# A Mamba layer with routed experts on one core: the skip term u*D scaled on ScalarE and added by turns on TensorE, batches 1 to 5

## Chip, cores and metric

One core of one Trainium2 chip. The metric is the device time of one execution in microseconds. The kernel before took 610.64 us, the median of 3 runs (609.68 to 610.68).

## What is computed

The input x is [8, 512, 128]: eight batches of 512 tokens. The layer returns x plus a Mamba block plus a mixture of experts, both on the normalised x. All arithmetic of the block is in fp32.

```python
xz = xn @ in_proj_w.T                       # x_s, z: 256 channels each
u = silu(causal_conv4(x_s) + conv_b)        # [b, t, 256]
delta = softplus(dt_raw @ dt_proj_w.T + dt_proj_b)
h = exp(delta * A) * h + delta * u * B_t    # 16 states per channel, a scan over t
y = sum over states of h * C_t  +  u * D_param
out = (y * silu(z)) @ out_proj_w.T + residual
```

The experts: two of eight for each token, each `(silu(x @ gate) * (x @ up)) @ down`, weighted and added. The change concerns the term `u * D_param`.

## The kernel before

**Layout.** Channels lie on the 128 partitions in two halves, hf = 0 and 1, and the 512 tokens of a batch along the free dimension. `u_sb[b % 3]` holds u of batch b as [128, 2, 512]; `d_sb` holds D_param as one column for each half.

**Order of the work.** Each engine has its own list, written out by hand, in batches b of 16 steps; step k is state k of the scan. In batches 1 to 5 one step has, on VectorE: the scan of half 0 (line 1144), the first gating product of an expert tile (line 1188), the product with C of half 0 (line 1161), the scan of half 1, the second gating product (line 1195), the product of half 1. ScalarE makes the decays exp(delta * A) into two PSUM banks by turns (`decay_bank`, line 515), each of which waits until the product that read the bank is done; it also moves the expert tile's results: `out_out` (line 714), `gate_out` (line 707) and `slots_out` (lines 696 and 700). Its list in a step is: decay of half 1, `out_out`, the work of `early`, the z gate in two steps, the decay of the next step's half 0, `gate_out`, `slots_out`, the work of `late`. In step 9 it takes the logarithm of the softplus for the next batch (line 770), with a table load before and another behind it, ahead of the decay of the next step and of `out_out`. Steps 8 and 14 have the two halves of tanh for the convolution of batch b + 2.

TensorE has in a step, in this order: the down projection of the tile before (`down`, line 1584), `up` (line 1598), `accumulate` (line 1433), the skip if there is one, `gate` (line 1592), `slots_turn` (line 1576), then convolutions, projections and the like. More exactly the skip of batches 1 to 5 comes once, in step 9 (`SKIP_AT`), behind `gate` and ahead of `slots_turn`; the latter waits for `out_out` of the tile before.

**Sum over states.** `accumulate` turns the products of one state (8 matmuls of 128x128 against the identity, with is_transpose) and adds them in two PSUM banks, `HT[0]` and `HT[1]`, which then hold y by time: tokens on partitions, channels along the free dimension. y stays there over the 16 steps.

**The skip.** `skip(b)` adds u * D_param into the same banks: 8 plain matmuls of u with `dd_sb[:, hf, :]`, a diagonal matrix of D_param that GpSimd makes at the start:

```python
MM(HT[i][:, t % 2, hf * P:(hf + 1) * P], u_sb[b % 3][:, hf, t * P:(t + 1) * P], dd_sb[:, hf, :],
   start=False, stop=False, skip_group_check=True)
```

Batches 0, 6 and 7 do it in other steps, in two parts. All of u_sb[b % 3] has other readers before step 6 of batch b only: the projection to B, C and dt (line 1482) and delta * u (line 457), both done for batch b while batch b - 1 runs. Its next writer is the convolution of batch b + 3.

**Other users of an engine's time.** `keep` (line 1341) issues matmuls whose result nobody reads; it stands in the steps of batches 0, 1, 5, 6 and 7 that have no expert tile. GpSimd makes dbu (line 931) and SyncE's queue brings expert weights, four tiles ahead, and rows of B and C.

Of the kernel before, what the change touches and what calls it, by code (L numbers as in the profile page):

```python
# [8 lines left out]
ACT = mybir.ActivationFunctionType  # L9
# [3 lines left out]
def build(nc, x, norm_w, w_in, conv_w, conv_b, x_proj, dt_proj, dt_b, a_log, d_par, w_out,  # L13
# [9 lines left out]
    P = 128  # L23
# [32 lines left out]
    with ctx:  # L56
        def sb(name, shape, dt=FP32):
            return ctx.enter_context(nc.sbuf_tensor(name, shape, dt))

        def sem(name):  # L60
            return ctx.enter_context(nc.semaphore(name))


        id_sb = sb("id_sb", [P, P])
# [8 lines left out]
        dd_sb = sb("dd_sb", [P, NH, P])  # L73
        dtb_sb = sb("dtb_sb", [P, NH])
        a_sb = sb("a_sb", [P, NH, S])
        d_sb = sb("d_sb", [P, NH])
# [52 lines left out]
        u_sb = [sb(f"u_sb{i}", [P, NH, T]) for i in range(3)]  # L129
# [27 lines left out]
                  for i in range(2)]  # L157
# [27 lines left out]
        HT = [bank[2 + q][:, :].rearrange("p (a c) -> p a c", a=2) for q in range(2)]  # L185
# [10 lines left out]
                   first1 first2 first3 first4 first5 first6 first7 both0 both1 both2 both3 both4 both5 both6 both7 part_mm comb dbuT_a sp_corr a_ready stats_bn st rms_rt xn_w xh_w  # L196
                   xh_pe xhT_c lgmm oh_out rt top_rdy sel_rdy tot_mm tot_out rk_out slot_rdy texp_rdy lohi_rdy lo_rdy hi_set hi_rdy map_mm src_rdy
                   exp_rt x_pad acc_w g_mm u_mm bct_rdy dbu_p row_mm dbu_0 b_st b_in0 b_in1 c_in0 c_in1
                   br_mm dbu_rdy da_rdy h_rdy p_rdy acc_mm y_out dd_rdy xc_mm x_th x_half u_rdy v_mm
                   v_out bc_mm bc_rdy z_mm z_rdy z_one o_ev sp_exp sp_ln sp_rem sp_w sp_sum z_th delta_rdy du_rdy  # L200
                   dut_mm dut_rdy yb_mm g_rdy o_mm o_rdy o_out""".split()
        s = {k: sem(k) for k in names}
# [12 lines left out]
        def tile(g):  # L215

            return TILE.get(g)
# [50 lines left out]
        def z_step(b):  # L268

            return {13: 1, 15: 0} if b == 0 else {7: 1, 11: 0} if b == 6 else {4: 1, 6: 0}  # L270
# [190 lines left out]
        def _(act):  # L461
# [32 lines left out]
            def decay(n):  # L494

                b, k = n // S, n % S
                i = IN_SBUF.index(n)
                for hf in range(NH):
                    if i >= ND:
                        act.wait_ge(s["h_rdy"], 2 * IN_SBUF[i - ND] + hf + 1)  # L500
                    if k == 0:
                        act.wait_ge(s["delta_rdy"], 2 * b + hf + 1)
                    nc.scalar.activation(da_of(n)[:, hf, :], delta[b % 2][:, hf, :], ACT.Exp,  # L503
                                         scale=a_sb[:, hf, k:k + 1]).then_inc(s["da_rdy"], 1)

            def decay_bank(n, hf):

                b, k = n // S, n % S
                m = 2 * k + hf
                wait(act, "p_rdy", freed(b, m))  # L510
                if b == 6 and m == 2:
                    act.wait_ge(s["dut_rdy"], 3)
                if k == 0:
                    act.wait_ge(s["delta_rdy"], 2 * b + hf + 1)
                nc.scalar.activation(bank_of(b, m)[:, :], delta[b % 2][:, hf, :], ACT.Exp,  # L515
                                     scale=a_sb[:, hf, k:k + 1]).then_inc(s["da_rdy"], 1)
# [18 lines left out]
            def input_turned(i):  # L535

                if i == 1:
                    act.wait_ge(s["o_rdy"], 5)
                for c in range(2):
                    act.wait_ge(s["dut_mm"], 2 * i + c + 1)  # L540
                    at = bank[2 + c] if i == 0 else FB[1 - c]
                    nc.scalar.activation(duT[:, 2 * c:2 * c + 2, :], at[:, :].rearrange("p (a c) -> p a c", a=2),
                                         ACT.Copy).then_inc(s["dut_rdy"], 1)
# [35 lines left out]
            def step(b, k):  # L579

                g = b * S + k
                prev, here, nxt, nn = tile(g - 1), tile(g), tile(g + 1), tile(g + 2)
                more = b < NB - 1
                if b < 6:
                    decay_bank(g, 1)
                elif b == 6:
                    if k == 0:
                        decay_bank(g, 1)
                        y_evac(b - 1)
                        input_turned(1)  # L590
                    if k + 1 < S and g + 1 not in BY_PE:
                        decay_bank(g + 1, 0)
                elif k == 0:
                    decay(g + 1)
                if k == 0 and b != 6:
                    y_evac(b - 1)
                if b == NB - 1 and k == TURNED + 2:
                    y_evac(b)
                if b == 7:
                    if k + 2 < S:  # L600
                        decay(g + 2)
                    if k == 0:
                        input_turned(2)
                    elif k + 1 < S:
                        scaled(g + 1)
                if b < 6 and k == LOG_AT[b]:
                    logarithm(b + 1)
                if prev is not None and not (b < 6 and k == LOG_AT[b]):
                    out_out(prev)
                if more:  # L610
                    early(b, k)
                if b != 6 and k in z_step(b):
                    z_gate(b, k)
                if b == 6 and k + 2 < S and g + 2 in BY_PE:
                    scaled(g + 2)
                if b < 6:
                    decay_bank(g + 1, 0)
                    if k == LOG_AT[b] and prev is not None:
                        out_out(prev)
                elif b == 6 and k + 1 < S and g + 1 not in BY_PE:  # L620
                    decay_bank(g + 1, 1)
                elif b == 6 and k + 1 == S:
                    decay_bank(g + 1, 0)
                    decay_bank(g + 1, 1)
                if nxt is not None:
                    gate_out(nxt)
                if nn is not None:
                    slots_out(nn)
                if b == 6 and k + 2 < S and g + 2 in BY_PE:
                    decay(g + 2)  # L630
                if more:
                    late(b, k)
                if b == 6 and k in z_step(b):
                    z_gate(b, k)

            def early(b, k):

# [22 lines left out]
            def z_gate(b, k):  # L660

                i, hf = z_turn(b, k), z_step(b)[k]
                if i == 0:
                    wait(act, "g_rdy", 2 * b)
                act.wait_ge(s["z_mm"], 2 * b + i + 1)
                if 0 < b < 6:
                    if i == 0:
                        act.wait_ge(s["z_rdy"], 2 * b)
                        wait(act, "o_rdy", b - 1)
                    if b == 1:  # L670
                        act.wait_ge(s["dbuT_a"], S - 1)
                    nc.scalar.activation(du_t[:, hf, :], z_bank(b)[:, :], ACT.Copy)
                nc.scalar.activation(zs_sb[:, hf, :], z_bank(b)[:, :], ACT.Tanh, scale=0.5).then_inc(s["z_th"], 1)
                if 0 < b < 6:
                    act.wait_ge(s["z_th"], 2 * b + i + 1)
                    nc.scalar.activation(zs_sb[:, hf, :], zs_sb[:, hf, :], ACT.Identity, bias=sign_sb[:, 0:1]).then_inc(s["z_one"], 1)

            def projected(b):

                act.wait_ge(s["o_mm"], b + 1)  # L680
                act.wait_ge(s["z_rdy"], 2 * b + 3)
                nc.scalar.activation(du_t[:, 1, :], FB[0][:, :], ACT.Copy).then_inc(s["o_ev"], 1)

            def y_evac(b):

                last = (b + 1) * S if b < NB - 1 else (NB - 1) * S + TURNED + 1
                for i in range(2):
                    wait(act, "acc_mm", 2 * last - 1 + i)
                    at = y_sb if b < NB - 1 else y_end
                    nc.scalar.activation(at[:, 2 * i:2 * i + 2, :], HT[i], ACT.Copy).then_inc(s["y_out"], 1)  # L690
# [643 lines left out]
        def _(pe):  # L1334
            MM = nc.tensor.matmul
# [102 lines left out]
            def skip(b, banks=(0, 1)):  # L1438

                if b == 0:  # L1440
                    pe.wait_ge(s["dd_rdy"], NH)
                for i in banks:
                    for t in (2 * i, 2 * i + 1):
                        for hf in range(NH):
                            last = MM(HT[i][:, t % 2, hf * P:(hf + 1) * P], u_sb[b % 3][:, hf, t * P:(t + 1) * P], dd_sb[:, hf, :],
                                      start=False, stop=False, skip_group_check=True)

            def conv(c, hf, taps):

# [273 lines left out]
            for hf in range(NH):  # L1723
# [3 lines left out]
               start=True, stop=True).then_inc(s["row_mm"], 1)  # L1727
# [15 lines left out]
            for hf in range(NH):  # L1743
                pe.wait_ge(s["g_rdy"], 2 * (NB - 1) + hf + 1)
                for i in range(2):
                    for t in (2 * i, 2 * i + 1):
                        last = MM((GB, UB)[i][:, (t % 2) * H:(t % 2 + 1) * H], g_sb[:, hf, t * P:(t + 1) * P], wo_sb[:, hf, :],
                                  start=False, stop=(hf == NH - 1), skip_group_check=True)
# [66 lines left out]
```

## Time and profile before

| | |
|---|---|
| median of 3 runs | 610.64 us (609.68 to 610.68) |
| profiled execution | 611.13 us, its span 609.3 us |
| VectorE (DVE) busy | 588.5 us, 97%, 852 instructions |
| TensorE (PE) busy | 542.0 us, 89%, 3554 |
| GpSimd (POOL) busy | 494.1 us, 81%, 389 |
| ScalarE (ACT) busy | 455.0 us, 75%, 916 |
| mean granted TensorE clock | 0.969 of full speed |

The span runs from the first to the last instruction; the profiled execution's time has 1.8 us more around it. Busy is the time in which the engine had an instruction running. Successive instructions of one engine overlap a little in the records, and a matmul's recorded length includes its way through the array. A fp32 matmul stands as several records where it needs several passes. L1445 is line 1445 of the kernel; "idle before" names what released the instruction.

### The profile page before, as it was taken

The page shows a single profiled execution, that of the slowest core. Times are in us where ns is not written, and L with a number is a line of the kernel's source. Part 1 is how long each engine was busy: PE and PEld are TensorE (multiplying, and loading weights), DVE is VectorE, ACT ScalarE, POOL GpSimd, SP SyncE. Part 2 cuts the span into 40 slices and gives each one's busy share as a digit, 9 for nine tenths or more (in the row PEclk, how much of TensorE's full clock was granted, in tenths as well). Part 3 has the DMA queues.
Part 4 walks back from the last instruction along what each step waited for, and adds up shares of the span by engine and source line. Part 5 has one row for each costly group of instructions (what it writes and reads, how often), then busy time and mean ns, then how long its engine had stood idle before and what let it go on. Part 6 is the DMA issues. An engine that isn't in the chain of part 4 may idle for free.

```text
span 609.3 us, 11382 instructions
## 1 busy us (share of the span) xinstructions
PE 542.0 (89%) x3554; PEld 422.5 (69%) x3554; DVE 588.5 (97%) x852; ACT 455.0 (75%) x916; POOL 494.1 (81%) x389
## 2 busy tenths in 40 slices
PE   5999889898898998999989999899999797778887
PEld 2387766656787777877887777877777465657564
DVE  6999989999999999999999999999999998999997
ACT  1789697259857888579876698767985589969880
POOL 5693466569999799998999889998998967885784
PEclk9889798979999999999999999999999899988999
DMA  7430119725787887878868888688884455333364
GB/s 205 135 130 1 74 36 223 306 82 157 256 304 223 293 289 223 311 226 296 296 190 304 291 288 279 203 300 268 280 266 156 156 195 210 110 99 98 88 137 90
DMA packets 60893, 122.99 MB, mean 202 GB/s; under 512 B 8218, under 2 KB 41378, under 8 KB 53794
## 3 DMA queue, kind: packets, MB, share of 16 engines
q1 hardware_dynamic: 53826, 112.42, 54.7%
q0 software_dynamic: 6288, 9.52, 7.3%
q8 instruction: 29, 0.48, 0.3%
q10 hardware_dynamic: 720, 0.33, 0.2%
q14 instruction: 30, 0.25, 0.1%
HBM read 112.77 MB, written 9.47 MB: 201 GB/s over the span
## 4 chain that ended last, share of the span: by engine, by line
PE 50%; DVE 19%; ACT 16%; issue 13%; POOL 1%; DMA 1%; DVEq 0%; ACTq 0%; POOLq 0%
PE bank L1433 9%; PE bank L1584 8%; PE bank L1467 8%; DVE bank L1144 8%; PE bank L1598 6%; DVE h_sb L1161 6%; PE bank L1592 5%; ACT bank L515 3%; ACT dbu L531 3%; PE bank L1490 2%; ACT da L503 2%; PE bank L1482 2%; PE bank L1396 1%; PE bank L1565 1%; ACT L770 1%
## 5 line engine op out<-in xcount | busy, mean ns | idle before, releaser
L931 POOL TENSOR_TENSOR dbu<-du,xn_all 128x1024 f32<-128x1024 f32 x86 | 203.7, 2369 | 24.9 <-DVE bank L1144 21.5
L1144 DVE TENSOR_TENSOR_SCAN bank<-bank,dbu 128x512 f32<-128x512 f32 x170 | 207.4, 1222 | 0.8 <-ACT bank L515 0.2
L1161 DVE TENSOR_TENSOR h_sb<-bank,xh_all 128x512 f32<-128x512 f32 x240 | 159.6, 680 | 1.2
L515 ACT ACTIVATE bank<-delta,a_sb 128x512 f32<-128x512 f32 x170 | 116.7, 688 | 37.9 <-DVE h_sb L1161 37.2
L1433 PE MATMUL bank<-id_sb,h_sb 128*128 128x128 f32 x992 | 131.9, 277 | 10.9 <-DVE h_sb L1161 9.3
L1433 PEld LDWEIGHTS bank<-id_sb,h_sb 128*128 128x128 f32 x992 | 112.9, 143 | 21.6 <-DVE h_sb L1161 14.7
L1144 DVE TENSOR_TENSOR_SCAN bank<-da,bank 128x512 f32<-128x512 f32 x82 | 96.0, 1215 | 4.6 <-PE bank L1396 2.9
L1584 PEld LDWEIGHTS bank<-wd_sb,hid 117*128 117x128 f32 (+1 forms) x432 | 54.8, 191 | 49.2 <-DVE hid L1195 28.4
L1584 PE MATMUL bank<-wd_sb,hid 117*128 117x128 f32 (+1 forms) x432 | 64.1, 284 | 18.7 <-ACT xT L696 17.2
L915 POOL DMA_INDIRECT xs<-xn_rows,src x72 | 69.8, 970 | 12.5 <-issue 9.9
L531 ACT ACTIVATE dbu<-du_t,bc_sb 128x256 f32<-128x256 f32 x164 | 69.4, 496 | 6.3 <-PE bank L1396 3.4
L1396 PE MATMUL bank<-id_sb,dbu 128*128 128x128 f32 x328 | 53.1, 288 | 15.1 <-DVE h_sb L1161 9.2
L1396 PEld LDWEIGHTS bank<-id_sb,dbu 128*128 128x128 f32 x328 | 39.6, 148 | 35.2 <-issue 23.7
L1467 PE MATMUL bank<-xhT,wk_sb 128*128 128x512 f32 x128 | 62.9, 619 | 0.7 <-ACT xhT L474 0.7
L503 ACT ACTIVATE da<-delta,a_sb 128x512 f32<-128x512 f32 x86 | 58.3, 714 | 5.0 <-DVE bank L1144 4.9
L1592 PE MATMUL bank<-xT,wgu_sb 128*118 128x128 f32 x432 | 59.3, 274 | 0.4 <-DVE ga L1188 0.2
L1598 PE MATMUL bank<-xT,wgu_sb 128*118 128x128 f32 x432 | 59.0, 272 | 0.0
L707 ACT ACTIVATE th<-bank 118x384 f32<-118x384 f32 x72 | 34.8, 483 | 26.8 <-PE bank L1592 25.9
L981 POOL DMA_INDIRECT xhT<-y_slots,slot x40 | 38.6, 965 | 19.0 <-DVE bank L1144 7.8
L1598 PEld LDWEIGHTS bank<-xT,wgu_sb 128*118 128x118 f32 x432 | 52.7, 182 | 0.5 <-issue 0.5
L1592 PEld LDWEIGHTS bank<-xT,wgu_sb 128*118 128x118 f32 x432 | 52.3, 182 | 0.9 <-issue 0.8
L714 ACT ACTIVATE ys<-bank,stat 128x128 f32<-128x128 f32 x72 | 26.2, 364 | 29.1 <-PE bank L1584 29.0
(198 smaller groups left out, 893.8 us busy)
## 6 DMA issues: line engine op xcount, KB each, us to landing
xh_all<-b_rows SPq DMA_DIRECT2D x30, 1024.0 KB, 7.5
xn_all<-b_rows SPq DMA_DIRECT2D x25, 1024.0 KB
wgu_sb<-in_w_gu SPq DMA_DIRECT2D x72, 352.0 KB
wd_sb<-in_w_dn SPq DMA_DIRECT2D x72, 192.0 KB
y_slots<-ys SPq DMA_DIRECT2D x72, 64.0 KB
xn_rows<-xn_all SPq DMA_DIRECT2D x2, 1040.0 KB, 11.4
out<-x_sb SPq DMA_DIRECT2D x7, 256.0 KB, 7.0
x_sb<-in_x SPq DMA_DIRECT2D x2, 640.0 KB, 6.0
```

Of the source, the lines that this page charges most:

```text
L503: nc.scalar.activation(da_of(n)[:, hf, :], delta[b % 2][:, hf, :], ACT.Exp, scale=a_sb[:, hf, k:k + 1]).then_inc(s["da_rdy"], 1)
L515: nc.scalar.activation(bank_of(b, m)[:, :], delta[b % 2][:, hf, :], ACT.Exp, scale=a_sb[:, hf, k:k + 1]).then_inc(s["da_rdy"], 1)
L531: last = nc.scalar.activation(dbuT[k % 2][:, t, :], duT[:, t, :], ACT.Copy, scale=bc_sb[q][:, t, k:k + 1])
L931: nc.gpsimd.tensor_tensor(dbu[k % 2][:, :, :], du[b % 2][:, :, :], b_ring[c % 2][:, k % CH, :].unsqueeze(1).to_broadcast([P, NH, T]), ALU. ...
L1144: nc.vector.tensor_tensor_scan(at, da_of(n)[:, hf, :] if n in IN_SBUF else at, inp, 0.0, ALU.mult, ALU.add).then_inc(s["h_rdy"], 1)
L1161: nc.vector.tensor_tensor(h_sb[k % 2][:, hf, :], bank_of(b, 2 * k + hf)[:, :], row, ALU.mult).then_inc(s["p_rdy"], 1)
L1396: last = nc.tensor.transpose(at[:, t * P:(t + 1) * P], dbuT[k % 2][:, t, hf * P:(hf + 1) * P], id_sb[:, :])
L1433: last = MM(HT[i][:, t % 2, hf * P:(hf + 1) * P], h_sb[k % 2][:, hf, t * P:(t + 1) * P], id_sb[:, :], is_transpose=True, start=(k == 0 and ...
L1467: last = MM(at[:, :], wk_sb[:, tap, hf * P:(hf + 1) * P], xhT[:, c, tap:tap + T], start=(tap == taps[0] if c == 0 else tap == 0), stop=(ta ...
L1584: last = MM(XD[:, P:P + H], hid[j % 2][0:FN[c], c * P:(c + 1) * P], wd_sb[j % NW][0:FN[c], c, :], start=(c == 0), stop=(c == NF - 1))
L1592: last = MM(GB[0:FW, c * P:(c + 1) * P], wgu_sb[j % NW][:, c * FS:c * FS + FW], xT[j % 2][:, :], start=True, stop=True)
L1598: last = MM(UB[0:FW, c * P:(c + 1) * P], wgu_sb[j % NW][:, F + c * FS:F + c * FS + FW], xT[j % 2][:, :], start=True, stop=True)
```

## The change

In batches 1 to 5, ScalarE multiplies u_sb[b % 3] in place by the column of D_param, one 128x512 half at the end of step 6 and one at the end of step 7. In step 9 TensorE waits for both and adds u with the identity and is_transpose, as `accumulate` does, in place of the product with the diagonal matrix. Batches 0, 6 and 7 stay as they are. A semaphore, `us_rdy`, is new.

```diff
@@ -632,6 +632,8 @@
                     late(b, k)
                 if b == 6 and k in z_step(b):
                     z_gate(b, k)
+                if 0 < b < 6 and k in (6, 7):
+                    skip_input(b, k - 6)
 
             def early(b, k):
 
@@ -680,6 +682,13 @@
                 act.wait_ge(s["o_mm"], b + 1)
                 act.wait_ge(s["z_rdy"], 2 * b + 3)
                 nc.scalar.activation(du_t[:, 1, :], FB[0][:, :], ACT.Copy).then_inc(s["o_ev"], 1)
+
+            def skip_input(b, hf):
+
+                act.wait_ge(s["br_mm"], b + 1)
+                act.wait_ge(s["du_rdy"], 2 * b + hf + 1)
+                nc.scalar.activation(u_sb[b % 3][:, hf, :], u_sb[b % 3][:, hf, :], ACT.Copy,
+                                     scale=d_sb[:, hf:hf + 1]).then_inc(s["us_rdy"], 1)
 
             def y_evac(b):
 
@@ -1439,11 +1448,14 @@
 
                 if b == 0:
                     pe.wait_ge(s["dd_rdy"], NH)
+                if 0 < b < 6:
+                    pe.wait_ge(s["us_rdy"], 2 * b)
                 for i in banks:
                     for t in (2 * i, 2 * i + 1):
                         for hf in range(NH):
-                            last = MM(HT[i][:, t % 2, hf * P:(hf + 1) * P], u_sb[b % 3][:, hf, t * P:(t + 1) * P], dd_sb[:, hf, :],
-                                      start=False, stop=False, skip_group_check=True)
+                            MM(HT[i][:, t % 2, hf * P:(hf + 1) * P], u_sb[b % 3][:, hf, t * P:(t + 1) * P],
+                               id_sb[:, :] if 0 < b < 6 else dd_sb[:, hf, :], is_transpose=0 < b < 6,
+                               start=False, stop=False, skip_group_check=True)
 
             def conv(c, hf, taps):
 
```

## Rows read from the trace of the kernel before

**Rows 1.** The page: busy us of each engine with shares of the span, and the granted clock

```profile
PE 542.0 (89%) x3554; PEld 422.5 (69%) x3554; DVE 588.5 (97%) x852; ACT 455.0 (75%) x916; POOL 494.1 (81%) x389
...
PEclk9889798979999999999999999999999899988999
```

**Rows 2.** A stretch within batches 1 to 5: length, busy us (instructions) PE, PEld, DVE, ACT, POOL, clock

```profile
140.00:470.00 330.00, 304.23 (x2261) 256.52 (x2260) 329.10 (x454) 257.75 (x543) 303.71 (x195) 1.00 0.78 263
```

**Rows 3.** Groups by form: line, engine, operation, count, busy us, mean ns of one

```profile
L1433 PE MATMUL bank<-id_sb,h_sb 128*128 128x128 f32 x992 | 131.9, 277 | 10.9 <-DVE h_sb L1161 9.3 <-DVE g_sb L1169 1.5
...
L1445 PE MATMUL bank<-dd_sb,u_sb 128*128 128x128 f32 x128 | 16.9, 284 | 0.0
...
L734 ACT ACTIVATE u_sb<-u_sb,sign_sb 128x512 f32<-128x512 f32 x14 | 10.1, 723 | 0.5
```

**Rows 4.** Timeline, ScalarE, batch 2, steps 6 to 8: start, length, instruction, idle before

```profile
224.48 0.38 ACT L700 ACTIVATE stat<-xs,stat 128x1 f32<-128x1 f32 x1
224.80 0.69 ACT L515 ACTIVATE bank<-delta,a_sb 128x512 f32<-128x512 f32 x1
225.67 0.37 ACT L714 ACTIVATE ys<-bank,stat 128x128 f32<-128x128 f32 x1 [0.18 <-PE bank L1584]
226.98 0.69 ACT L515 ACTIVATE bank<-delta,a_sb 128x512 f32<-128x512 f32 x1 [0.94 <-DVE h_sb L1161]
...
229.16 0.69 ACT L515 ACTIVATE bank<-delta,a_sb 128x512 f32<-128x512 f32 x1 [0.38 <-DVE h_sb L1161]
230.35 0.37 ACT L714 ACTIVATE ys<-bank,stat 128x128 f32<-128x128 f32 x1 [0.50 <-PE bank L1584]
```

**Rows 5.** Timeline, VectorE, batch 2, steps 7 to 11

```profile
226.87 1.22 DVE L1144 TENSOR_TENSOR_SCAN bank<-bank,dbu 128x512 f32<-128x512 f32 x1
...
231.23 1.22 DVE L1144 TENSOR_TENSOR_SCAN bank<-bank,dbu 128x512 f32<-128x512 f32 x1
...
238.62 1.23 DVE L1144 TENSOR_TENSOR_SCAN bank<-bank,dbu 128x512 f32<-128x512 f32 x1
...
246.41 0.54 DVE L1195 TENSOR_TENSOR hid<-ga,bank 118x384 f32<-118x384 f32 x1
```

**Rows 6.** Timeline, ScalarE, batch 2, step 9

```profile
233.53 0.69 ACT L515 ACTIVATE bank<-delta,a_sb 128x512 f32<-128x512 f32 x1
...
237.90 0.69 ACT L515 ACTIVATE bank<-delta,a_sb 128x512 f32<-128x512 f32 x1
238.53 0.35 ACT L714 ACTIVATE ys<-bank,stat 128x128 f32<-128x128 f32 x1
```

**Rows 7.** Timeline, TensorE, batch 2, steps 9 to 11

```profile
236.28 1.95 PE L1445 MATMUL bank<-dd_sb,u_sb 128*128 128x128 f32 x16
239.02 0.30 PE L1576 MATMUL bank<-id_sb,xs 128*128 128x128 f32 x1 [0.79 <-ACT ys L714]
239.78 0.91 PE L1584 MATMUL bank<-wd_sb,hid 117*128 117x128 f32 x6 [0.46 <-ACT xT L696]
...
241.18 1.04 PE L1433 MATMUL bank<-id_sb,h_sb 128*128 128x128 f32 x8
...
245.27 0.82 PE L1598 MATMUL bank<-xT,wgu_sb 128*118 128x128 f32 x6
```

**Rows 8.** Stretches: batches 6 and 7, columns as in rows 2

```profile
479.00:483.00 4.00, 1.77 (x10) 0.86 (x8) 3.97 (x5) 2.39 (x5) 3.53 (x4) 1.00 0.26 57
483.10:486.40 3.30, 3.27 (x10) 2.10 (x10) 2.78 (x5) 2.75 (x5) 3.13 (x3) 0.50 0.75 290
513.80:517.40 3.60, 1.60 (x12) 1.28 (x12) 2.18 (x4) 3.57 (x8) 2.97 (x4) 1.00 1.00 397
517.40:521.00 3.60, 2.96 (x19) 2.05 (x20) 3.60 (x5) 3.60 (x8) 2.64 (x4) 1.00 0.33 120
547.90:551.20 3.30, 1.32 (x10) 0.99 (x10) 3.07 (x4) 3.30 (x8) 0.39 (x2) 1.00 0.08 20
551.40:554.70 3.30, 3.30 (x15) 2.96 (x14) 3.30 (x5) 3.22 (x7) 2.41 (x3) 0.50 0.17 43
```

More of the change, by code:

```diff
@@ L198, in build @@
                    exp_rt x_pad acc_w g_mm u_mm bct_rdy dbu_p row_mm dbu_0 b_st b_in0 b_in1 c_in0 c_in1
-                   br_mm dbu_rdy da_rdy h_rdy p_rdy acc_mm y_out dd_rdy xc_mm x_th x_half u_rdy v_mm
+                   br_mm us_rdy dbu_rdy da_rdy h_rdy p_rdy acc_mm y_out dd_rdy xc_mm x_th x_half u_rdy v_mm
                    v_out bc_mm bc_rdy z_mm z_rdy z_one o_ev sp_exp sp_ln sp_rem sp_w sp_sum z_th delta_rdy du_rdy
```

## Prediction

> **What bounds the kernel now.** I read the page first. VectorE is busy for 97% of the span, TensorE for 89%, ScalarE for 75% [rows 1]. Such a share is a mean over unlike stages, so the second view is the table of stretches. Over 330 us inside batches 1 to 5, the only batches that the change touches, VectorE is busy for 329.10 us: it idles 0.9 us in all, with TensorE at 304.23, ScalarE at 257.75, and a granted clock of 1.00 throughout [rows 2]. These batches end when VectorE has done its list. Time taken off another engine there is worth nothing by itself; time put on another engine costs only what it makes VectorE wait. The third view is the timeline of one batch (batch 2; the other four repeat it within 0.1 us), read for slack: how late may ScalarE and TensorE be before VectorE notices?
>
> **The change, part by part.**
>
> *Eight matmuls become eight turns, per batch.* A product of fp32 operands is recorded as two matmuls, a turn as one: 128 records of line 1445 are 64 products, while line 1433 has one record for each turn [rows 3]. The skip block of batch 2 is 16 records in 1.95 us; eight turns of the same shape take 1.04 us [rows 7]. TensorE is done 0.91 us sooner, five times: 4.5 us of its work is gone. But the skip is followed by an idle time of 0.79 us, which ends only when ScalarE has moved the expert output (line 714) [rows 7], and line 714 stands behind the logarithm and its two table loads, which put the next decay at 237.90 and line 714 at 238.53 [rows 6]. Neither depends on TensorE being done with the skip. So the 0.91 us turns into idle time, 1.70 us instead of 0.79. **Value: 0.** Its cover is the logarithm on ScalarE.
>
> *Ten multiplications on ScalarE.* I price one by the nearest row, the in-place 128x512 of line 734: 0.72 us [rows 3], 7.2 us in all. They stand at the end of steps 6 and 7. The first comes after the small operation at 224.48 and ahead of the decay at 224.80 [rows 4]. That decay moves to 225.52 and ends at 226.21; its scan starts at 226.87 [rows 5], so 0.66 us are left. The evacuation behind it (225.67) ends by 226.6, and the decay after that waits for VectorE until 226.98 anyway [rows 4]. The lateness ends there. The second stands ahead of the decay at 229.16, which comes after 0.38 us of idle time, so from 228.78 to 229.50; the decay ends at 230.19, its scan starts at 231.23, and the evacuation at 230.35 waits for TensorE [rows 4, 5]. From 230.35 on ScalarE is as it was. That matters: the decay at 233.53 starts the logarithm chain, whose end (237.90 plus 0.69) already sets the scan at 238.62 [rows 5, 6]. **Value: 0**, with 7.2 us as the end on the other side, if no cover held. The copy is of the kind that line 531 makes between Exps, and I expect no table load.
>
> *The waits.* The turns wait for both multiplications, done some 6 us before the skip. The multiplications wait for things of the batch before. Nothing queues behind either; no DMA moves, except that the store of the expert output in step 7 leaves some 0.6 us later, with three tiles of weights in hand behind it. **Value: 0.**
>
> *What the longer idle time does to TensorE's clock.* Here I expect the cost. With the change TensorE ends the skip at about 237.3, does one turn at 239.02, waits again 0.46 us, and resumes at 239.78 [rows 7]: 0.3 us of work in 2.5 us, where before it had 1.2 us. The rows before a low clock look like that. From 479.00 to 483.00 PE did 10 matmuls, busy 1.77 us, and the next 3.3 us were granted at 0.50, 1.2 GHz in place of 2.4. From 547.90 to 551.20 it was 10 matmuls and 1.32 us, and again 0.50 followed. From 513.80 to 517.40 it was 12 matmuls and 1.60 us, and the clock stayed at 1.00 [rows 8]. From 236.3 to 239.8 the changed kernel would have 12 matmuls at most, and from 237.3 to 240.8 about ten: among those that fell. In batches 1 to 5 of the kernel before no such thin stretch exists. TensorE's timeline has seven idle times of 1.5 us or more behind the start, all outside batches 1 to 5, and four were followed by the low clock. So I count half of the five skips, 2.5 falls.
>
> Price of a fall: the low clock lasts about 3.3 us in each case [rows 8], and it begins some microseconds after the gap, on the unbroken work from 239.78 to 246.1. At half speed 3.3 us hold 1.65 us of work, so the up projection at 245.27, ending at 246.09, is 1.65 us late. VectorE needs it at 246.41 [rows 5, 7]: slack 0.32. A fall costs 1.65 - 0.32 = 1.3 us, between 0.8 (if another idle time takes part of it) and 1.65 (no slack). VectorE never wins it back, having no idle time.
>
> **Sum.** 0 + 0 + 0 + 2.5 x 1.3 = +3.3 us. The profiled execution took 611.13 us (span 609.3); the median of the runs is 610.64, 0.5 below. On the median: 613.9 us.
>
> A rule of the Trainium skill speaks against this change more strongly. Row first: all 12 matmuls from 513.80 to 517.40 are turns (lines 1396 and 1433), and the clock stayed at 1.00 [rows 8]. The page "TensorE: Matmul & The Clock Gate", section "Part 4: PE-mode transpose", says that a transpose does not count as TensorE activity as a matmul does. By that rule the skip would lose all its weight and all five batches would fall; by the row, turns count about as the others do. I take the row, and keep the rule as a rival.
>
> **The rivals.**
>
> A, the forecast: the clock falls after two or three of the five skips, 613.9 us (2 to 4 falls: 613.2 to 615.8). Chance 0.55.
>
> B, not slower: the clock holds. The place is the stretch from 237.3 to 240.8; it decides whether its ten matmuls keep the clock up. For it: the stretch at 513.80, and that nine of the ten are records of products, where rows 8 are mostly turns. Against it: both falls of rows 8 came after ten. Price 0, so 610.6 us. Chance 0.31.
>
> C, every batch falls, in that turns weigh nothing or the gap alone suffices: 5 x 1.3 = 6.5, so 617.1 us. Against it: rows 8 at 513.80. The page's rule named above is this case. Chance 0.06.
>
> D, ScalarE becomes late: the multiplications push the logarithm chain, 2 x 0.72 us in each of five batches at worst, 617.8 us. It decides at the 0.66 us and at 230.35; the timeline says that both hold. Chance 0.03.
>
> E, TensorE is the true bound, as the chain of waits with its half on PE would have it: 0.91 us back in each batch, 606.1 us. Against it: VectorE's 0.9 us of idle time in 330. Chance 0.04. It also holds the case that the clock of batches 6 and 7 falls differently and gives time back.
>
> F: the turns are recorded and run as products, so nothing is saved and no gap opens: 610.6 us. Line 1433 makes the same accumulating turn, so chance 0.01.
>
> **How the numbers follow.** Slower by over 0.2% (1.2 us, about what a measurement of this kernel can tell from no change): A, C and D, 0.64; a single fall at 1.3 us would already count. Within 0.2%: B and F, 0.32. Faster: E, 0.04. The range reaches from B's end, 610.3, to four falls at 1.3 us, 615.8; it leaves out C, D and E, 0.13. A's own range is 612.2 (two falls at 0.8 us) to 615.8.
>
> **What would show it.** Line 1445 has 88 records instead of 128. A new ScalarE line has ten operations of about 0.72 us. The idle time before line 1576 after each skip grows from 0.79 to about 1.7 us. Where A holds, a stretch at 0.50 stands inside batches 1 to 5, some 3.4 to 8 us after a skip, and after it the products of line 1195 come 1.3 us late, with VectorE idle and TensorE as the releaser. If the clock is 1.00 there and the five batches keep their length, B holds and my price of the gap was wrong. If VectorE's decays come late in steps 7 and 8, D holds.

## The result and the profile after

The change made the kernel slower: 615.82 us, the median of 7 runs (613.67 to 619.0), beside 611.37 us for the kernel before on the same chips (7 runs). The ratio is 1.0079, 95% interval 1.0056 to 1.0102, so +4.8 us. The forecast was 613.9 us, slower by clock falls; direction and mechanism hold, the size came out too small: +3.3 us forecast, +4.8 us measured. The 615.82 us lies 0.02 us above the range, which was worked out from 610.64 us; the kernel before, timed again beside the changed one, was itself 0.7 us slower than that.

First the page of the changed kernel, its busy times and granted clock:

```profile
PE 539.5 (88%) x3514; PEld 421.5 (69%) x3514; DVE 589.8 (96%) x852; ACT 459.6 (75%) x926; POOL 494.0 (80%) x389
...
PEclk9899798979999998999999999899998999989999
```

VectorE's busy time is little changed (589.8 us, 588.5 in [rows 1]); the span grew from 609.3 to 614.5 us. The clock row has an eight in the sixteenth slice, the twenty-sixth and the thirty-first, inside the batches where [rows 1] have only nines.

The groups by form (line, engine, operation, count, busy us, mean ns of one, idle before): the skip and the new operation.

```profile
L1588 PE MATMUL bank<-id_sb,xs 128*128 128x128 f32 x72 | 20.1, 279 | 8.0 <-ACT ys L723 8.0
...
L1456 PE MATMUL bank<-dd_sb,u_sb 128*128 128x128 f32 x48 | 7.8, 318 | 0.0
...
L690 ACT ACTIVATE u_sb<-u_sb,d_sb 128x512 f32<-128x512 f32 x10 | 7.2, 716 | 0.0
...
L1456 PE MATMUL bank<-id_sb,u_sb 128*128 128x128 f32 x40 | 5.2, 273 | 0.0
```

Line 1456 has 48 + 40 = 88 records instead of the 128 of [rows 3], and the turned ones took 5.2 us for all five batches. The ten multiplications (line 690) took 716 ns each, 7.2 us in all. TensorE idled 8.0 us ahead of the turns of line 1588, which wait for ScalarE's line 723. The records and the price of a multiplication are as forecast from [rows 3].

The table of stretches (length, busy of PE, PEld, DVE, ACT, POOL, clock), three short ones and most of batches 1 to 5:

```profile
241.90:245.20 3.30, 3.30 (x18) 3.30 (x17) 3.13 (x5) 1.01 (x3) 3.12 (x3) 0.50 0.77 213
388.70:392.00 3.30, 3.30 (x18) 3.30 (x17) 2.98 (x5) 1.14 (x3) 3.12 (x3) 0.50 0.86 211
463.80:467.10 3.30, 3.30 (x18) 3.30 (x17) 3.11 (x4) 0.56 (x1) 2.23 (x1) 0.50 0.64 226
150.00:470.00 320.00, 291.76 (x2136) 246.74 (x2135) 315.60 (x434) 251.59 (x533) 289.07 (x186) 0.98 0.79 263
```

Three stretches at half clock, where the kernel before has none from 150 to 470 us. They stand behind the skips of batches 2, 4 and 5. VectorE's idle time in 320 us is 320 - 315.60 = 4.4 us; in the kernel before it was 0.9 in 330 [rows 2].

**One fall in the timeline.** TensorE of the changed kernel in batch 2:

```profile
237.85 1.04 PE L1456 MATMUL bank<-id_sb,u_sb 128*128 128x128 f32 x8
240.50 0.30 PE L1588 MATMUL bank<-id_sb,xs 128*128 128x128 f32 x1 [1.61 <-ACT ys L723]
241.25 1.05 PE L1596 MATMUL bank<-wd_sb,hid 117*128 117x128 f32 x6 [0.46 <-ACT xT L705]
...
248.41 0.82 PE L1610 MATMUL bank<-xT,wgu_sb 128*118 128x128 f32 x6
...
257.02 0.82 PE L1610 MATMUL bank<-xT,wgu_sb 128*118 128x128 f32 x6
...
261.71 0.82 PE L1610 MATMUL bank<-xT,wgu_sb 128*118 128x128 f32 x6
```

The skip now ends at 238.9, TensorE idles 1.61 us instead of 0.79 [rows 7], and at 241.88 the clock falls. The up projection of step 11 starts at 248.41. Batch 2 begins 1.48 us later than in the kernel before, so undisturbed it would have started at 246.75: it is 1.66 us late. VectorE in the same place:

```profile
239.24 0.74 DVE L1184 SCALAR_TENSOR_TENSOR u_sb<-bank,cb_sb,u_sb 128x512 f32<-128x512 f32 x1
240.10 1.23 DVE L1153 TENSOR_TENSOR_SCAN bank<-bank,dbu 128x512 f32<-128x512 f32 x1
...
243.68 0.56 DVE L1204 TENSOR_TENSOR hid<-ga,bank 118x384 f32<-118x384 f32 x1 [0.17 <-issue]
...
246.57 0.56 DVE L1197 SCALAR_TENSOR_TENSOR ga<-th,bank 118x384 f32<-118x384 f32 x1 [0.60 <-ACT th L716]
...
249.32 0.56 DVE L1204 TENSOR_TENSOR hid<-ga,bank 118x384 f32<-118x384 f32 x1 [0.46 <-issue]
...
262.62 0.56 DVE L1204 TENSOR_TENSOR hid<-ga,bank 118x384 f32<-118x384 f32 x1
...
263.69 0.74 DVE L1184 SCALAR_TENSOR_TENSOR u_sb<-bank,cb_sb,u_sb 128x512 f32<-128x512 f32 x1
...
470.43 0.56 DVE L1204 TENSOR_TENSOR hid<-ga,bank 118x384 f32<-118x384 f32 x1 [0.40 <-issue]
```

Up to 240.10 VectorE is 1.48 us behind the kernel before, the offset that it brought along from batch 1 (more on this at the end of the account of the prediction). The gating product that stood at 246.41 [rows 5] now stands at 249.32, so 2.91 us behind: 1.43 us lost. Up to there it waits three times: 0.17, 0.60 and 0.46 us of visible idle time. The waits of VectorE, grouped, from 150 to 470 us (total, times, longest):

```profile
DVE ga L1197 <- ACT th L716: 1.9, 3, 0.8
DVE hid L1204 <- issue: 1.4, 4, 0.5
DVE bank L1153 <- ACT bank L515: 0.6, 1, 0.6
```

All but the last row come from late work of TensorE (line 716 itself waits for TensorE's gate projection); "issue" in front of line 1204 is read here as the wait for the up projection, whose end the profile only models: after each of these waits line 1204 starts 0.09 us behind that end (248.41 + 0.82 = 249.23, then 249.32).

### The profile page after: what moved, and what is told of

The parts are those of the page before. It is cut to its first block, busy times and chain, and to the rows that moved or that the text cites. A ratio compares the mean times of both kernels' runs of the same rounds, so it can differ in the third digit from the quotient of the medians.

```text
span 614.5 us, 11322 instructions
## 1 busy us (share of the span) xinstructions
PE 539.5 (88%) x3514; PEld 421.5 (69%) x3514; DVE 589.8 (96%) x852; ACT 459.6 (75%) x926; POOL 494.0 (80%) x389
## 4 chain that ended last, share of the span: by engine, by line
PE 49%; ACT 18%; DVE 17%; issue 14%; POOL 1%; DMA 1%; ACTq 0%; DVEq 0%; POOLq 0%
PE bank L1442 10%; PE bank L1596 8%; PE bank L1479 7%; PE bank L1610 6%; DVE bank L1153 6%; PE bank L1604 5%; DVE h_sb L1170 5%; ACT bank L515 3%; ACT dbu L531 3%; PE bank L1502 2%; ACT da L503 2%; PE bank L1494 2%; PE bank L1577 1%; PE bank L1405 1%; ACT L779 1%
## 5 line engine op out<-in xcount | busy, mean ns | idle before, releaser
L1442 PE MATMUL bank<-id_sb,h_sb 128*128 128x128 f32 x992 | 136.7, 283 | 13.4 <-DVE h_sb L1170 10.9
L1442 PEld LDWEIGHTS bank<-id_sb,h_sb 128*128 128x128 f32 x992 | 116.6, 146 | 24.9 <-DVE h_sb L1170 16.6
L1405 PEld LDWEIGHTS bank<-id_sb,dbu 128*128 128x128 f32 x328 | 38.2, 145 | 37.7 <-issue 26.0
L1610 PE MATMUL bank<-xT,wgu_sb 128*118 128x128 f32 x432 | 60.5, 277 | 0.0
L1604 PE MATMUL bank<-xT,wgu_sb 128*118 128x128 f32 x432 | 60.5, 277 | 0.0
L1610 PEld LDWEIGHTS bank<-xT,wgu_sb 128*118 128x118 f32 x432 | 54.0, 185 | 0.5 <-issue 0.5
L1604 PEld LDWEIGHTS bank<-xT,wgu_sb 128*118 128x118 f32 x432 | 54.0, 187 | 0.1
```

Of the source, the lines that this page charges most:

```text
L1405: last = nc.tensor.transpose(at[:, t * P:(t + 1) * P], dbuT[k % 2][:, t, hf * P:(hf + 1) * P], id_sb[:, :])
L1442: last = MM(HT[i][:, t % 2, hf * P:(hf + 1) * P], h_sb[k % 2][:, hf, t * P:(t + 1) * P], id_sb[:, :], is_transpose=True, start=(k == 0 and ...
L1604: last = MM(GB[0:FW, c * P:(c + 1) * P], wgu_sb[j % NW][:, c * FS:c * FS + FW], xT[j % 2][:, :], start=True, stop=True)
L1610: last = MM(UB[0:FW, c * P:(c + 1) * P], wgu_sb[j % NW][:, F + c * FS:F + c * FS + FW], xT[j % 2][:, :], start=True, stop=True)
```

## The experiments

Each was timed in 3 to 5 rounds beside the kernel before. The first four ran together on one chip, where the kernel before took 611.21 us, and the last three on another, where it took 611.16 us. In batches 1 to 5 the second adds u without D_param, the third adds the term twice, the fourth adds it for half of the channels and the fifth leaves it out.

### Multiplications without the shorter skip

```diff
-  id_sb[:, :] if 0 < b < 6 else dd_sb[:, hf, :], is_transpose=0 < b < 6,
+  id_sb[:, :] if 0 < b < 6 else dd_sb[:, hf, :], is_transpose=False,
```

> The change with its ten multiplications on ScalarE, but the skip again as 8 plain products (16 records), of the scaled u with the identity. Clock theory (the shorter skip lets TensorE's clock fall afterwards, and that is all the cost): the time of the kernel before, within 1.2 us, no granted clock of 0.50 between 150 and 470 us, line 1576 again idle some 0.8 us after the skip. ScalarE theory (the multiplications make decays or the logarithm late): the changed kernel's time, some 4.8 us above the kernel before, at a full clock.

Measured: ratio 0.9994 (0.9979 to 1.001), 611.13 us. The stretch from 150 to 470 us, and the idle time behind the skip:

```profile
150.00:470.00 320.00, 295.96 (x2196) 249.40 (x2195) 319.06 (x439) 252.61 (x533) 294.55 (x189) 1.00 0.79 265
...
238.01 0.30 PE L1588 MATMUL bank<-id_sb,xs 128*128 128x128 f32 x1 [0.79 <-ACT ys L723]
```

The clock is 1.00, VectorE's idle time 0.9 us, the gap 0.79 us, with all ten multiplications made. The multiplications cost nothing that these rounds could tell: the ScalarE theory falls.

### The shorter skip without multiplications

```diff
-                if 0 < b < 6 and k in (6, 7):
-                    skip_input(b, k - 6)
...
-                if 0 < b < 6:
-                    pe.wait_ge(s["us_rdy"], 2 * b)
```

> The 8 turns of the change without the multiplications: the skip adds u, not u times its weight, in batches 1 to 5. Clock theory: the changed kernel's time, 4 to 5.5 us above the kernel before, with two or three stretches at 0.50 some 3 to 8 us after a skip, and VectorE held up 1.5 to 1.7 us behind each. ScalarE theory: the time of the kernel before, within 1.2 us.

Measured: 1.0077 (1.0055 to 1.0099), 615.9 us, the changed kernel's time. Three stretches at half clock, behind the skips of batches 1, 2 and 4:

```profile
168.00:171.30 3.30, 3.30 (x18) 3.30 (x17) 3.00 (x6) 1.14 (x3) 3.12 (x4) 0.50 0.72 213
243.10:246.40 3.30, 3.30 (x18) 3.30 (x17) 3.11 (x4) 0.56 (x1) 3.13 (x4) 0.50 0.90 285
389.90:393.20 3.30, 3.30 (x18) 3.30 (x17) 3.24 (x4) 0.69 (x2) 3.12 (x4) 0.50 0.84 230
```

The turns alone bring the whole loss. Together with the first experiment this settles which half of the change costs.

### Sixteen turns

```diff
-                        for hf in range(NH):
+                        for hf in (0, 0, 1, 1) if 0 < b < 6 else range(NH):
```

> The change with every turn of the skip made twice (16 turns, u counted twice in batches 1 to 5): as long on TensorE as the 16 records of the kernel before, but turns alone. If turns weigh like other matmuls for the clock: no 0.50 between 150 and 470 us, and the time of the kernel before within 1.2 us. If turns do not count as activity (the Trainium skill, page TensorE: Matmul & The Clock Gate, Part 4: PE-mode transpose): stretches at 0.50 behind the skips as in the changed kernel or more of them, 4.8 us or more above the kernel before.

Measured: 0.9995 (0.9978 to 1.0012), 610.63 us.

```profile
150.00:470.00 320.00, 295.69 (x2199) 249.08 (x2198) 319.05 (x438) 252.23 (x530) 294.61 (x188) 1.00 0.79 264
...
234.09 1.91 PE L1456 MATMUL bank<-id_sb,u_sb 128*128 128x128 f32 x16
236.83 0.30 PE L1588 MATMUL bank<-id_sb,xs 128*128 128x128 f32 x1 [0.83 <-ACT ys L723]
```

Sixteen turns fill 1.91 us, the gap is 0.83 us again, and the clock stays at 1.00 in all five batches. So it is not the form: sixteen turns held the clock up as well as sixteen records of products did. The rule of the Trainium skill, page "TensorE: Matmul & The Clock Gate", section "Part 4: PE-mode transpose", is not borne out for these fp32 turns.

### Half of the products

The kernel before, with the channels of half 0 only in its skip:

```diff
-                        for hf in range(NH):
+                        for hf in range(1 if 0 < b < 6 else NH):
```

> The kernel before with half of the skip left out in batches 1 to 5 (channels of half 0 only): 8 records of plain products, no turn, nothing new on ScalarE. If the amount of TensorE work ahead of the gap decides: the changed kernel's time, 4 to 5.5 us above the kernel before, with two or three stretches at 0.50. If it is the kind of work (turns in place of products) that decides: fewer falls than in the changed kernel, none or one, under 2 us above the kernel before.

Measured: 1.0053 (1.0032 to 1.0074), 614.76 us. Four stretches at half clock, behind the skips of batches 1, 2, 4 and 5:

```profile
165.00:168.30 3.30, 3.17 (x15) 3.20 (x16) 2.56 (x5) 1.79 (x4) 3.14 (x2) 0.50 0.60 194
240.10:243.40 3.30, 3.30 (x18) 3.30 (x17) 3.25 (x5) 0.95 (x2) 3.13 (x3) 0.50 0.81 211
386.90:390.20 3.30, 3.30 (x18) 3.30 (x17) 3.12 (x5) 1.02 (x3) 3.13 (x3) 0.50 0.71 205
462.00:465.30 3.30, 3.30 (x18) 3.30 (x17) 3.04 (x5) 1.09 (x3) 1.47 (x1) 0.50 0.19 62
...
238.58 0.30 PE L1576 MATMUL bank<-id_sb,xs 128*128 128x128 f32 x1 [1.58 <-ACT ys L714]
```

Eight records of plain products lose the clock like eight turns, with the same gap, here 1.58 us. How much TensorE does there decides, not the kind of work. Whether it is the work ahead of the gap or the length of the gap is not separated: in every experiment here less of the one comes with more of the other. The loss of 3.2 us by the ratio is less than the 4 to 5.5 us expected, and the profile has one stretch more than the two or three expected. In this profile VectorE also lost 0.9 us in batch 5 ahead of its fall, at full clock and mostly behind late decays; why is open.

### No skip at all

```diff
-                if 0 < b < NB - 2 and k == SKIP_AT:
-                    skip(b)
```

> The kernel before without the skip in batches 1 to 5 (the term u times its weight is left out there): 16 records less ahead of the gap of step 9, nothing new on ScalarE. TensorE's work falls by 1.9 us in each batch. Clock theory: slower, not faster: TensorE idles some 2.5 us where it idled 0.8, so the 0.50 follows at least as often as in the changed kernel, 3 to 5 times, at 1.5 to 1.7 us each, 4.8 to 8 us above the kernel before. A theory in which TensorE's amount of work bounds the batches: up to 9 us faster. A theory in which only the form or the operands of the turns cost: the time of the kernel before.

Measured: 1.0061 (1.0037 to 1.0084), 614.51 us. TensorE has 80 records less, five blocks of the 1.95 us of [rows 7], and the kernel is slower for it. Three skips' places were followed by the low clock (the first twice as long as the others), and the gap is 2.47 us:

```profile
165.60:172.30 6.70, 5.70 (x25) 5.46 (x26) 5.71 (x8) 2.86 (x8) 6.52 (x5) 0.50 0.59 159
315.80:319.10 3.30, 3.30 (x17) 3.30 (x17) 3.30 (x5) 0.95 (x2) 3.13 (x4) 0.50 0.68 196
462.60:465.80 3.20, 3.20 (x17) 3.20 (x17) 3.14 (x5) 0.95 (x2) 1.60 (x1) 0.50 0.43 156
...
241.51 0.30 PE L1576 MATMUL bank<-id_sb,xs 128*128 128x128 f32 x1 [2.47 <-ACT ys L714]
```

It fell no more often than in the changed kernel, though the gap is 0.9 us longer. In batches 2 and 4, which kept the clock, the time from unit product to unit product was 22.77 and 22.78 us, beside 22.78 and 22.84 us in the kernel before: TensorE's 1.95 us less gave nothing back. The lower end of what I expected held for the number, and the time is 1 us below what I gave.

### The changed kernel again

> The changed kernel as it is, for another profile of it. Clock theory: two to four stretches at 0.50 between 150 and 470 us, not all behind the same skips as in the first profile, each with VectorE held up 1.4 to 1.7 us, and 4 to 5.5 us above the kernel before.

Measured: 1.0053 (1.0028 to 1.0077), 614.08 us. This profile has its low clock behind the skips of batches 1, 2 and 4:

```profile
168.00:171.30 3.30, 3.30 (x18) 3.30 (x17) 3.07 (x5) 1.04 (x3) 3.22 (x3) 0.50 0.74 216
243.10:246.40 3.30, 3.30 (x18) 3.30 (x17) 3.01 (x4) 0.53 (x2) 3.13 (x4) 0.50 0.84 249
389.90:393.10 3.20, 3.20 (x17) 3.20 (x16) 3.12 (x4) 0.57 (x1) 3.02 (x4) 0.50 0.87 248
```

The interval overlaps the first one's; the two put the loss at 3.2 and 4.8 us. The 3.2 us is below the 4 to 5.5 us expected. Over the five profiles with a shorter skip or none the low clock followed 3, 3, 4, 3 and 3 of five places. It is not evenly spread: in the four profiles with a shorter skip it came behind batches 2 and 4 every time and behind batch 3 never, while without any skip it came behind 1, 3 and 5. Executions without a kept profile may have had fewer: two of the ten timings of this kernel, 611.43 and 611.89 us, are as fast as the kernel before, at a mean granted clock of 0.980 where the profiled one had 0.961.

### Clock kept up elsewhere

The kernel before with seven matmuls whose result nobody reads, in idle times away from the skips, at the starts of batches 1, 6 and 7:

```diff
+                    if b == 6:
+                        keep(GB[:, :])
+                    elif b == 7:
+                        pe.wait_ge(s["comb"], 1)
+                        for _ in range(3):
+                            keep(UB[:, :])
                     accumulate(g - 1)
                     if b == 1:
+                        for _ in range(2):
+                            keep(MAP[:, 2 * NJ:], False)
                         inverse(6)
...
+                if b == 7 and k == 1:
+                    keep(UB[:, :])
```

> The kernel before with matmuls that nobody reads put into four idle times of TensorE outside the batches of the change: two of 128x368 at the start of batch 1, one, three and one of 128x512 at the start of batch 6, at that of batch 7 and in step 1 of batch 7. They end before the wait that follows them does. If the clock is worth time there too: the falls near 121, 483, 544 and 551 us go away, and the kernel is 1 to 3 us faster than the kernel before. If VectorE hides those falls: the same time within 1.2 us.

Measured: 0.9992 (0.9973 to 1.0011), 610.01 us: no difference that can be told. From 140 to 600 us, this kernel and then the kernel before:

```profile
140.00:600.00 460.00, 413.51 (x2929) 333.81 (x2928) 456.31 (x605) 362.09 (x745) 404.84 (x276) 1.00 0.69 226
```

```profile
140.00:600.00 460.00, 411.74 (x2914) 334.74 (x2913) 454.85 (x604) 362.09 (x745) 403.36 (x275) 0.99 0.69 226
```

The falls near 121, 483, 544 and 551 us are gone, and VectorE idles 3.7 us instead of 5.2 in this stretch. Less idle time in one profile did not become time in the runs. The falls that the kernel before has in its profile cost it little; none of these versions beats it beyond the noise.

## Why the prediction was right in kind and short in size

**TensorE's saved time is worth nothing: right.** The saving became idle time, 1.61 us in batch 2 instead of 0.79 (forecast: 1.70), and likewise in all five batches (1.55 to 1.62 instead of 0.64 to 0.80). Without any skip at all the batches did not get shorter either.

**Ten multiplications are covered: right.** ScalarE of the changed kernel, batch 2 (1.48 us behind the kernel before by its start):

```profile
226.32 0.71 ACT L690 ACTIVATE u_sb<-u_sb,d_sb 128x512 f32<-128x512 f32 x1
226.94 0.68 ACT L515 ACTIVATE bank<-delta,a_sb 128x512 f32<-128x512 f32 x1
...
230.86 0.69 ACT L515 ACTIVATE bank<-delta,a_sb 128x512 f32<-128x512 f32 x1
...
235.00 0.69 ACT L515 ACTIVATE bank<-delta,a_sb 128x512 f32<-128x512 f32 x1
...
239.38 0.69 ACT L515 ACTIVATE bank<-delta,a_sb 128x512 f32<-128x512 f32 x1
```

The first multiplication at 226.32 puts the decay at 226.94 instead of 226.28, which is 224.80 [rows 4] plus the offset; the second puts its decay at 230.86 instead of 230.64. The decay ahead of the logarithm is at 235.00, again only the offset behind its 233.53, and the one behind the chain at 239.38 [rows 6]. So they came 0.66 and 0.22 us late, of the 0.72 and 0.34 forecast, and nothing behind them did. The first experiment shows the same for the whole kernel.

**The clock falls behind the shortened skip: right.** The stretches at 0.50 begin 3.9 to 4.7 us behind the start of the skip, on the unbroken work, and last some 3.4 us. Four experiments pin it down: the loss is there with turns alone and with half of the products alone, and it is gone as soon as TensorE's old amount of work stands ahead of the gap.

**How often: forecast 2.5 of five, shown three, in one kernel four.** I took half from seven idle times in other batches, of very different kinds; that it came near is luck. That was the first term mis-sized. Skips that differ only in when they come, some 73 us apart, fared differently in the same profile, and batches 2 and 4 fell in each profile of a shorter skip; what picks them is not shown.

**What one costs: forecast 1.3 us, measured 1.6.** This is the step that failed. I took the slack of 0.32 us at step 11 and let VectorE pay the rest. It did pay 1.43 there. There the slack is 0.32 less the 0.09 us by which line 1204 follows the up projection even when it waits for it: 0.23 us, and 1.66 - 0.23 = 1.43. But TensorE has not made up its lateness by then, and in steps 12 and 13, which have a convolution, it needs longer for a step (257.02 to 261.71, 4.69 us) than VectorE (4.36 us, [rows 5]). TensorE of the kernel before there:

```profile
253.88 0.82 PE L1598 MATMUL bank<-xT,wgu_sb 128*118 128x128 f32 x6
...
258.56 0.82 PE L1598 MATMUL bank<-xT,wgu_sb 128*118 128x128 f32 x6
```

Its up projection of step 13 ends at 258.56 + 0.82 = 259.38, and VectorE needs it at 259.50 (below): the slack has shrunk to 0.12 by the forecast's way of counting, and to 0.03 once the 0.09 us are taken off. TensorE is still 1.67 us late (261.71, less 258.56 and the offset of 1.48), so VectorE should be 1.64 us late, and it is: line 1204 stands at 262.62, 3.12 us behind 259.50, of which 1.48 are the offset. VectorE of the kernel before in the same places, with the unit products on either side:

```profile
237.77 0.74 DVE L1175 SCALAR_TENSOR_TENSOR u_sb<-bank,cb_sb,u_sb 128x512 f32<-128x512 f32 x1
...
259.50 0.54 DVE L1195 TENSOR_TENSOR hid<-ga,bank 118x384 f32<-118x384 f32 x1
...
260.55 0.74 DVE L1175 SCALAR_TENSOR_TENSOR u_sb<-bank,cb_sb,u_sb 128x512 f32<-128x512 f32 x1
...
464.24 0.54 DVE L1195 TENSOR_TENSOR hid<-ga,bank 118x384 f32<-118x384 f32 x1
```

From unit product to unit product it takes 22.78 us before (237.77 to 260.55) and 24.45 after (239.24 to 263.69): the fall of batch 2 cost 1.67 us. The same difference is 1.62 us in batch 4, 1.45 in batch 5 and 0.00 in batch 3, which kept its clock. Batch 5 fits the account: its last product of line 1195 is the one at 464.24, two steps behind the skip like the one at 246.41, so it has no step of the small slack and pays the first instalment alone (470.43 less 464.24 and an offset of 4.76 is 1.43). Three falls make 4.74 us. Sized so, the sum would have been 2.5 x 1.5 = 3.8, or 3 x 1.5 = 4.5 us, and four falls at 1.6 would have put the range's end at 617.0.

**The rivals.** B, where the clock holds, did not happen in any profile of the short skip; the two fast timings of the changed kernel may be such cases. C, every batch, is refuted in its form by the sixteen turns; even no skip lost the clock at three places only. D, ScalarE late, is refuted by the first experiment; E, TensorE as the bound, by the one without a skip; F by the 88 records.

One loss in the profile after comes before the change can act: at the start of batch 1, ahead of the first new instruction (153.75 us), VectorE went from 1.3 us ahead of the kernel before to 1.2 us behind, with the clock at 0.50 for 10 us from 129.24 on; the kernel before has 7 us of it, from 121.26 on, and its VectorE waits for no more than 0.13 us at a time behind that. A stretch at 0.50 from about 130 us stands in the three profiles of kernels with eight turns and in none of the other six, though all these programs but the last experiment's are alike up to there; what sets it, and whether it is chance, is open. So the profile's 5.2 us of longer span is 4.7 us of falls and 0.5 us of such differences, most of which cancel. The second experiment, which has no multiplication, also lost 0.5 us behind the logarithm of batch 1, as the changed kernel did; ScalarE's new work is not the cause of that.

## What to carry to other kernels

Work taken from TensorE just ahead of a wait isn't free where another engine is the bound: it can cost the clock of the stretch behind the wait. Ask of every removed matmul how long TensorE then idles and how full the work after it is; if a cheaper form opens a gap, the old form, or useless matmuls of the same length, may be the faster choice; here doubling the turns gave the time back, 610.63 us beside 611.21 us. And follow a lateness through to the step with the least slack, not to the first one.

## What was not expected

Removing 1.9 us of matmuls per batch instead of 0.9 lost the clock no more often: 3 of five places at a gap of 2.47 us, 3 or 4 at one of 1.6. Filling TensorE's gaps in batches 1, 6 and 7 removed every stretch at 0.50 behind 140 us and was worth no time that five rounds could tell (0.9992, interval 0.9973 to 1.0011): those stretches cost no time that shows. But a low clock away from the skips is not free in general: VectorE lost 2.5 us behind the one at 129.24 us, in which TensorE was busy for nearly all of it. What tells the two apart may be whether TensorE's work behind the fall is unbroken up to the point that VectorE waits for; no experiment here tests that.
